# A deformable-convolution block: the first pair's weight products ahead of the second pair's offset convolution, batch norm operations and second grid later on DVE

## Chip, cores and metric

One NeuronCore of a Trainium2 chip runs one program. The metric is the device time of one execution, in microseconds (us); lower is better. Engines are named as in the profile: PE (TensorE; PEld its weight loads), DVE (VectorE), ACT (ScalarE), POOL (GpSimd), SP (SyncE, whose queue issues most DMAs).

## What is computed

Two residual bottleneck blocks on x of shape (4, 256, 16, 16). Only the middle of the first is touched by the change: a 3x3 convolution gives offsets and a mask, a deformable 3x3 convolution samples with them.

```python
out = relu(group_norm(conv(x, w1)))                # 64 channels
om = conv(out, w_off, pad=1) + b_off               # 27 channels
off_x, off_y, mask = om[:, :9], om[:, 9:18], sigmoid(om[:, 18:])
py, px = grid_y + off_y, grid_x + off_x
sampled = bilinear_sample(out, py, px) * mask      # 9 taps
out = einsum('bckhw,ock->bohw', sampled, w2)
out = relu(group_norm(out)); out = group_norm(conv(out, w3)); x = relu(out + x)
# second block: 16-bit quantised activations, power-of-two weights:
# 1x1, depthwise 3x3, batch norm, relu, 3x3, batch norm, relu, 1x1, batch norm, + x, relu
```

## The kernel before

The four images are laid out as two pairs (`b2` 0 and 1); within a pair the two images are the halves `h`, on partitions 0 to 63 and 64 to 127. Every engine has its program written out by hand, and semaphores are all that orders the engines against each other. An engine runs its own list strictly in order.

Bilinear sampling is done as matrix products. A **unit** `i` (0 to 7) is a tile `t = i // 2` (pair `t // 2`, 128 of its 256 pixels) and a half `h`. For each tile DVE makes `differences(t)` (offset coordinate minus pixel coordinate) and from them the hat functions `hats`, in y and x; `apply_mask(t)` multiplies the sigmoid mask into one of them. For each unit `make_g(i)` multiplies the two hats out into `g_rows` (9 taps by 256 source pixels), called g(i) below. PE transposes it in thirds of three taps, `turn(n)`, into one of the three double banks `slot`, ACT copies each third to `g_cols` (`copy_g(n)`), and PE multiplies `g_cols` with `v_sb` and sums into `acc` (`sample(t, first_tap, last_tap)`). For tiles 0 and 1 DVE makes the hats alone; for tiles 2 and 3 ACT does the second half of it (`distance(2)`, `distance(3)`), between its copies.

`v_sb` holds the **weight products**: features times w2, eight products v0 to v7 (`make_v(i)`, 128x512, eight taps of one pair, pixel half and image) and eight small ones for the ninth tap (`make_last_v(i)`). A product uses 64 rows of the PE array, those of its half `i % 2`. PE writes them to PSUM, ACT copies them (`copy_v(i)`, and two copies for the ninth tap).

The **offsets** of a pair: `om_step(b2, s)` (five steps) is the offset convolution; of its result ACT copies the upper 64 partitions (`copy_om_rest`), and DVE adds the grid to the lower ones (`add_grid`). `om_turn(b2)` transposes the sum on PE; its result is copied to `omt_sb` (DVE for the first pair, ACT in `copy_omt(1)` for the second), and ACT makes the mask. In the kernel before, PE runs both offset convolutions one after the other with `om_turn(0)` inside the second, then v0 to v3, `om_turn(1)`, and the rest of the products, and only then the turns. The second pair's offsets lie in the second banks of `slot[0]` and `slot[1]`.

The six **batch norm operations** (`bn_std`, `bn_inv`, `bn_off`, `bn_minus`) are DVE work on 128x4 elements or less, needed only in the second block. In the kernel before they stand right after `add_grid(0)`.

Later on DVE: `moments(0)` and `pair_scale(3, 0)` normalise the first pair, five operations quantise the weights (`wq_mag`, `wqb`), and `eight_moments(0)` takes the moments of `conv3(0)`; PE waits for these in `eight_means(0)`, between two stretches of sampling of tile 3.

Of the kernel before, what the change touches and what calls it, by code (L numbers as in the profile page):

```python
# [38 lines left out]
P = 128  # L39
# [75 lines left out]
def build(nc, x, first, pairs, consts, woff, grid, w2, w3, wq, out):  # L115
    with ExitStack() as ctx:
# [233 lines left out]
        def _(pe):  # L350
# [35 lines left out]
            def om_step(b2, s):  # L386
                for p in range(2):
                    k = s + TAPS_A * p
                    if k < TAPS:
                        mm = nc.tensor.matmul(slot[0][CB * p:CB * p + CB, BANK * b2:BANK * b2 + N],  # L390
# [4 lines left out]
            def om_turn(b2):  # L395
# [10 lines left out]
            for b2 in range(B2):  # L406
                pe.wait_ge(feat_ready, b2 + 1)
                for s in range(TAPS_A):
                    mm = om_step(b2, s)
                    if b2 == 1 and s == 1:  # L410
                        pe.wait_ge(consts_in, 16)
                        om_turn(0)
                mm.then_inc(om_done, 1)

            v_banks = [small[0], small[1], acc[0][:], acc[1][:]]
            pe.wait_ge(w2_in, 16)

            def make_v(i):  # L420
                b2, q, h = i // 4, i // 2 % 2, i % 2
                pe.wait_ge(flat_ready, b2 + 1)
                if i >= 4:

                    pe.wait_ge(v_ready, i - 3)
                at = N * b2 + P * q
                lhs = feat_flat[rows(h), at:at + P]
                nc.tensor.matmul(v_banks[i % 4], lhs, w2_sb[rows(h), 0:BANK], start=True, stop=True
                                 ).then_inc(v_done, 1)

            def make_last_v(i):
                b2, q, h = i // 4, i // 2 % 2, i % 2
# [12 lines left out]
            mm.then_inc(v_done, 1)


            def turn(n):
# [176 lines left out]
        def _(a):  # L625
# [587 lines left out]
```

## Time and profile before

| what | value |
|---|---|
| time, median of 3 runs (lowest to highest) | 92.92 us (92.44 to 93.06) |
| time of the profiled execution | 93.05 us |
| its span in the trace | 91.27 us |
| PE, DVE, ACT busy | 75.5, 67.0, 51.1 us |

The span is what the trace shows between first and last instruction; the time has some 1.8 us around it. Busy times overlap, since the engines run side by side. Matmuls are pipelined and their ends are modelled. The trace leaves buffer numbers out, so `w_sb` is w2 or w3, and `slot` any of the three.

### The profile page before, as it was taken

Reading aid. Unit: us, or ns where it says so; the run is one execution under the profiler, and the core shown is the slowest. Engines: PE = TensorE matmul, PEld = TensorE weight load, DVE = VectorE, ACT = ScalarE, POOL = GpSimd, SP = SyncE. Lnnn points to the kernel's source line nnn. Section 1 sums busy time; section 2 is a strip of 40 time slices with the busy share of each in tenths; the row PEclk is TensorE's granted clock in tenths of the full one; section 3 lists DMA queues with packets and bytes.
Section 4 is the critical chain, followed back from the end, with each engine's and each line's share of the span. In section 5 each row is a group of like instructions: output and inputs, shape, how many; then the busy total and the mean of one; then the engine's idle time right before and its main releaser. Section 6 shows DMA issues by size and latency. Waiting matters only on the chain.

```text
span 91.3 us, 2176 instructions
## 1 busy us (share of the span) xinstructions
PE 75.5 (83%) x886; PEld 51.3 (56%) x886; DVE 67.0 (73%) x182; ACT 51.1 (56%) x92; POOL 5.0 (6%) x10
## 2 busy tenths in 40 slices
PE   4999999995899898999999989967359889896400
PEld 1325665564798878798996964452214385572100
DVE  1225449999999599995799437977898875849950
ACT  4102374879948999994792015336363343744760
POOL 7500110000000000000003100000000000000000
PEclk9999999999999999999999999999999999999975
DMA  1999800000000000000000000000000000000076
GB/s 21 317 337 292 334 4 0 0 0 7 0 7 0 0 7 0 7 7 0 0 7 0 0 0 7 0 0 0 0 0 0 0 0 0 7 4 0 0 245 215
DMA packets 3274, 4.17 MB, mean 46 GB/s; under 512 B 256, under 2 KB 2688, under 8 KB 3264
## 3 DMA queue, kind: packets, MB, share of 16 engines
q1 hardware_dynamic: 2992, 3.76, 12.8%
q10 hardware_dynamic: 272, 0.26, 0.8%
q8 instruction: 7, 0.11, 0.5%
q14 instruction: 3, 0.02, 0.1%
HBM read 2.98 MB, written 1.05 MB: 44 GB/s over the span
## 4 chain that ended last, share of the span: by engine, by line
PE 49%; DVE 32%; ACT 10%; issue 4%; DVEq 0%; ACTq 0%
PE acc L475 15%; PE slot L462 9%; DVE g_rows L886 8%; PE slot L354 6%; PE acc L604 5%; PE acc L365 3%; DVE g_cols L1040 3%; PE slot L390 3%; ACT g_cols L704 2%; DVE g_cols L984 2%; ACT g_cols L788 2%; PE slot L539 2%; ACT pad L757 2%; DVE g_cols L1130 2%; DVE stats L948 2%
## 5 line engine op out<-in xcount | busy, mean ns | idle before, releaser
L886 DVE TENSOR_TENSOR g_rows<-hats 128x2304 f32<-128x2304 f32 (+1 forms) x12 | 20.6, 1752 | 0.1
L704 ACT ACTIVATE g_cols<-slot 128x768 f32<-128x768 f32 x24 | 17.8, 830 | 3.7 <-PE slot L462 3.7
L475 PE MATMUL acc<-g_cols,v_sb 128*64 128x128 f32 x288 | 17.9, 277 | 0.0
L475 PEld LDWEIGHTS acc<-g_cols,v_sb 128*64 128x64 f32 x288 | 15.5, 137 | 1.1 <-issue 0.3
L354 PE MATMUL slot<-zeros 128*128 128x512 bf16 x54 | 15.1, 412 | 1.2 <-DVE zeros L807 1.2
L462 PE MATMUL slot<-consts_sb,g_rows 64*128 64x64 f32 x288 | 11.8, 226 | 2.1 <-DVE g_rows L886 1.7
L462 PEld LDWEIGHTS slot<-consts_sb,g_rows 64*128 64x128 f32 x288 | 10.3, 139 | 3.9 <-DVE g_rows L886 2.6
L354 PEld LDWEIGHTS slot<-zeros 128*128 128x128 bf16 x54 | 5.4, 107 | 7.3 <-issue 2.6
L757 ACT ACTIVATE pad<-g_cols 64x256 bf16<-64x256 int8 x8 | 3.3, 418 | 4.6 <-DVE g_cols L1040 4.5
L817 DVE BATCH_NORM_STATS2 stats<-acc 128x6 f32<-128x256 f32 x4 | 1.7, 428 | 5.2 <-PE acc L365 2.6
L539 PE MATMUL slot<-consts_sb,mx 128*128 128x128 f32 x12 | 3.2, 319 | 2.3 <-DVE mx L991 2.0
L390 PE MATMUL slot<-feat,woff_sb 128*64 128x256 f32 x36 | 4.7, 385 | 0.0
L635 ACT ACTIVATE std<-var,eps_sb 128x1 f32<-128x1 f32 x4 | 1.2, 297 | 6.1 <-DVE var L824 6.1
L539 PEld LDWEIGHTS slot<-consts_sb,mx 128*128 128x128 f32 x12 | 1.8, 176 | 4.0 <-DVE mx L991 2.5
L780 ACT ACTIVATE act<-raw,bn_off 128x256 f32<-128x256 f32 x4 | 2.0, 508 | 2.8 <-DVE mx L1116 2.8
L390 PEld LDWEIGHTS slot<-feat,woff_sb 128*64 128x64 f32 x36 | 2.7, 135 | 1.2
L734 ACT ACTIVATE g_cols<-g_cols 128x512 f32<-128x512 f32 x2 | 1.3, 631 | 3.6 <-DVE piece_max L984 3.6
L1116 DVE CUSTOM_DVE_ANT_0 raw<-acc,bn_mul,bn_minus 128x256 f32<-128x256 f32 x4 | 1.9, 482 | 1.7 <-DVE bn_mul L1124 0.9
L345 POOL TENSOR_TENSOR pegq<-consts_sb,wqb 128x576 bf16<-128x576 f32 x1 | 1.1, 1149 | 37.2 <-DVE wqb L942 37.2
L757 ACT ACTIVATE g_cols<-g_cols 128x512 bf16<-128x512 int8 x4 | 2.4, 625 | 1.3 <-DVE g_cols L1040 1.2
L855 DVE TENSOR_TENSOR hats<-omt_sb,consts_sb 128x576 f32<-128x576 f32 x4 | 3.0, 752 | 0.0
L984 DVE CUSTOM_DVE_ANT_0 g_cols<-g_cols,x_sb 128x256 f32<-128x256 f32 x8 | 3.0, 417 | 0.1
(140 smaller groups left out, 117.6 us busy)
## 6 DMA issues: line engine op xcount, KB each, us to landing
out<-g_cols SPq DMA_DIRECT2D x4, 256.0 KB, 2.3
x_sb<-x SPq DMA_DIRECT2D x3, 256.0 KB, 4.4
wq_sb<-wq SPq DMA_DIRECT2D x1, 484.5 KB, 6.3
woff_sb<-woff SPq DMA_DIRECT2D x1, 288.0 KB, 5.5
w_sb<-w SPq DMA_DIRECT2D x1, 288.0 KB, 5.5
x_sb<-x ACTq DMA_DIRECT2D x1, 256.0 KB, 3.1
w_sb<-w SPq DMA_DIRECT2D x1, 256.0 KB, 6.4
consts_sb<-consts SPq DMA_DIRECT2D x1, 232.0 KB, 5.4
```

The source lines that it names most:

```text
L354: nc.tensor.matmul(bank, zeros[:, 0:P], zeros[:], start=True, stop=True)
L365: mm = nc.tensor.matmul(acc[b2][rows(h), 0:N], w1_sb[:, c, :], x_sb[:, c, b2, h, :], start=(c == 0), stop=(c == CH - 1))
L390: mm = nc.tensor.matmul(slot[0][CB * p:CB * p + CB, BANK * b2:BANK * b2 + N], woff_sb[:, k, :], window(feat, b2, k), start=(s == 0), stop= ...
L462: mm = nc.tensor.transpose(slot[SLOT_OF[n % TURNS]][:, BANK * r + at:BANK * r + at + CB], g_rows[i % 3][rows(r), k, ROWS_Q * q:ROWS_Q * q ...
L475: mm = nc.tensor.matmul(acc[b2][rows(h), at:at + P], v_sb[:, B2 * h + b2, q, k, :], g_cols[t][h][:, NQ * k + q, :], start=(k == 0 and q == ...
L539: nc.tensor.matmul(spread[b2] if biased else small[b2][:, P:2 * P], mx[:, n, b2:b2 + 1].to_broadcast([P, P]), ident, start=not biased, sto ...
L604: mm = nc.tensor.matmul(acc[b2][rows(h), 0:N], weights(k), window(pad[:, b2], h, k), start=(k == 0), stop=(k == TAPS - 1))
L704: nc.scalar.activation(dst.rearrange("p k (r n) -> p k r n", r=HALVES), src.rearrange("p r (k n) -> p k r n", k=per), ACT.Copy).then_inc(g ...
L757: nc.scalar.activation(dst, src, ACT.Copy, scale=256.0).then_inc(hi_ready, 1)
L855: return tt(hats[:, t].rearrange("p h a k y -> p h (a k) y"), omt_sb[:, t // NQ, t % NQ, :, 0:2 * TAPS].unsqueeze(3).to_broadcast([P, HALV ...
L886: tt(g_rows[i % 3][:, taps], hats[:, t, h, 1, taps].unsqueeze(3).to_broadcast(shape), hats[:, t, h, 0, taps].unsqueeze(2).to_broadcast(sha ...
L984: last = nc.vector.tensor_tensor_reduce(y0[:, c, b2, h, :], y0[:, c, b2, h, :], x_sb[:, c, b2, h, :], 1.0, 0.0, ALU.add, ALU.max, piece_ma ...
```

## The change

On PE, v0 now comes before `om_turn(0)`, then v1 to v3 and all eight ninth-tap products; the second pair's offset convolution comes after v4, with v5 after its third step and v6 behind it. `om_turn(1)` moves behind `sample(0, 0, 4)`, and v7 behind `sample(0, 5, 6)`. The wait for w2's transfer moves ahead of the first offset convolution. The second pair's offsets and their transpose go to the bank `acc[1]`; v4, v5 and v6 use `acc[0]`, v7 `acc[1]`. The ninth-tap products go to the first banks of `slot[0]` and `slot[1]`. ACT's copies follow that order. On DVE the batch norm operations move behind `pair_scale(3, 0)`, and `add_grid(1)` behind `make_g(1)`. No instruction is added or taken away.

```diff
+        def om_of(b2, p):
+            return (slot[0] if b2 == 0 else acc[1])[rows(p), 0:N]
+        def omt_of(b2):
+            return (slot[1] if b2 == 0 else acc[1])[:, 0:NQ * CB]
+        v_banks = (small[0], small[1], acc[0][:], acc[1][:], acc[0][:], acc[0][:], acc[0][:], acc[1][:])
+        def last_v_of(h):
+            return slot[h][:, 0:T * CB]
...
             pe.wait_ge(woff_in, 16)
-            for b2 in range(B2):
-                pe.wait_ge(feat_ready, b2 + 1)
-                for s in range(TAPS_A):
-                    mm = om_step(b2, s)
-                    if b2 == 1 and s == 1:
-                        pe.wait_ge(consts_in, 16)
-                        om_turn(0)
-                mm.then_inc(om_done, 1)
-            v_banks = [small[0], small[1], acc[0][:], acc[1][:]]
             pe.wait_ge(w2_in, 16)
             def make_v(i):
                 b2, q, h = i // 4, i // 2 % 2, i % 2
                 pe.wait_ge(flat_ready, b2 + 1)
-                if i >= 4:
-                    pe.wait_ge(v_ready, i - 3)
                 at = N * b2 + P * q
                 lhs = feat_flat[rows(h), at:at + P]
-                nc.tensor.matmul(v_banks[i % 4], lhs, w2_sb[rows(h), 0:BANK], start=True, stop=True
+                nc.tensor.matmul(v_banks[i], lhs, w2_sb[rows(h), 0:BANK], start=True, stop=True
                                  ).then_inc(v_done, 1)
             def make_last_v(i):
                 b2, q, h = i // 4, i // 2 % 2, i % 2
-                at = BANK * h + CB * (i // 2)
-                return nc.tensor.matmul(slot[0][:, at:at + CB], feat_flat[rows(h), N * b2 + P * q:N * b2 + P * q + P],
+                at = CB * (i // 2)
+                return nc.tensor.matmul(last_v_of(h)[:, at:at + CB], feat_flat[rows(h), N * b2 + P * q:N * b2 + P * q + P],
                                         w2_sb[rows(h), BANK:TAPS * CB], start=True, stop=True)
-            for i in range(4):
-                make_v(i)
-            om_turn(1)
-            for i in range(4):
-                make_last_v(i)
-            for i in range(4, 2 * T):
-                make_v(i)
+            pe.wait_ge(feat_ready, 1)
+            for s in range(TAPS_A):
+                mm = om_step(0, s)
+            mm.then_inc(om_done, 1)
+            make_v(0)
+            pe.wait_ge(consts_in, 16)
+            om_turn(0)
+            make_v(1)
+            make_v(2)
+            pe.wait_ge(feat_ready, 2)
+            make_v(3)
+            pe.wait_ge(omt_ready, 1)
+            pe.wait_ge(flat_ready, B2)
+            for i in range(2 * T):
                 mm = make_last_v(i)
             mm.then_inc(v_done, 1)
+            pe.wait_ge(v_ready, 3)
+            make_v(4)
+            pe.wait_ge(v_ready, 4)
+            for s in range(TAPS_A):
+                mm = om_step(1, s)
+                if s == 2:
+                    pe.wait_ge(v_ready, 6)
+                    make_v(5)
+            mm.then_inc(om_done, 1)
+            pe.wait_ge(v_ready, 7)
+            make_v(6)
...
-                    pe.wait_ge(v_ready, (5, 6, 2 * T + 1)[n])
+                    pe.wait_ge(v_ready, 5)
...
             turns(0, 5)
             sample(0, 0, 4)
+            om_turn(1)
             turns(6, 8)
             sample(0, 5, 6)
+            pe.wait_ge(omt_ready, 2)
+            make_v(7)
...
             copy_om_rest(0)
             nc.scalar.preload_act_table(ACT.Sigmoid)
             make_mask(0)
-            copy_om_rest(1)
-            for i in range(2 * T):
+            for i in range(4):
                 copy_v(i)
-                if i == 3:
-                    copy_omt(1)
-            a.wait_ge(v_done, 2 * T + 1)
+            a.wait_ge(v_done, 5)
             for h in range(HALVES):
                 last = nc.scalar.activation(v_sb[:, B2 * h:B2 * h + B2, :, V_MAIN, :],
-                                            slot[0][:, BANK * h:BANK * h + T * CB].rearrange(
-                                                "p (b q o) -> p b q o", b=B2, q=NQ), ACT.Copy)
+                                            last_v_of(h).rearrange("p (b q o) -> p b q o", b=B2, q=NQ), ACT.Copy)
             last.then_inc(v_ready, 1)
+            for i in range(4, 7):
+                copy_v(i)
+            copy_om_rest(1)
...
+                if n == 5:
+                    copy_omt(1)
                 if n == 8:
+                    copy_v(7)
                     distance(2)
...
             add_grid(0)
-            dve.wait_ge(bn_std_ready, 1)
-            settle(nc.vector.reciprocal(bn_std[:], bn_std[:]))
-            settle(tt(bn_inv[:], bn_std[:], vec[:, V_BNG:V_BNG + 4], ALU.mult))
-            settle(tt(bn_off[:], bn_inv[:], vec[:, V_BNM:V_BNM + 4], ALU.mult))
-            settle(tt(bn_off[:], vec[:, V_BNB:V_BNB + 4], bn_off[:], ALU.subtract))
-            settle(stt(bn_off[:, 0:1], bn_inv[:, 0:1], vec[:, V_PEGB:V_PEGB + 1], bn_off[:, 0:1], ALU.mult, ALU.add))
-            settle(ts(bn_minus[:], bn_off[:, 0:2], -1.0, None, ALU.mult))
             dve.wait_ge(omt_done, 1)
-            nc.vector.tensor_copy(omt_sb[:, 0].rearrange("p q h o -> p (q h o)"), slot[1][:, 0:NQ * CB]
+            nc.vector.tensor_copy(omt_sb[:, 0].rearrange("p q h o -> p (q h o)"), omt_of(0)
                                   ).then_inc(omt_ready, 1)
             settle(differences(0))
             make_hats(0)
-            add_grid(1)
             apply_mask(0)
             make_g(0)
             make_g(1)
+            add_grid(1)
             settle(differences(1))
             make_hats(1)
             apply_mask(1)
...
             pair_scale(3, 0, V_GN2S, V_GN2B)
+            dve.wait_ge(bn_std_ready, 1)
+            settle(nc.vector.reciprocal(bn_std[:], bn_std[:]))
+            settle(tt(bn_inv[:], bn_std[:], vec[:, V_BNG:V_BNG + 4], ALU.mult))
+            settle(tt(bn_off[:], bn_inv[:], vec[:, V_BNM:V_BNM + 4], ALU.mult))
+            settle(tt(bn_off[:], vec[:, V_BNB:V_BNB + 4], bn_off[:], ALU.subtract))
+            settle(stt(bn_off[:, 0:1], bn_inv[:, 0:1], vec[:, V_PEGB:V_PEGB + 1], bn_off[:, 0:1], ALU.mult, ALU.add))
+            settle(ts(bn_minus[:], bn_off[:, 0:2], -1.0, None, ALU.mult))
             dve.wait_ge(wq_in, 16)
...
```

PE around the offset convolutions, before (`feat,woff_sb` is the convolution, `consts_sb,om_sb` is `om_turn`, `w2_sb,feat_flat` a weight product, 128x512 a large one, 128x64 a ninth-tap one):

```order
L390 MATMUL slot0<-feat,woff_sb 64x256 [waits feat_ready,woff_in]
L390 MATMUL slot0<-feat,woff_sb 64x256 x8
L390 MATMUL slot0<-feat,woff_sb 64x256 [waits feat_ready]
L390 MATMUL slot0<-feat,woff_sb 64x256 x3
L401 MATMUL slot1<-consts_sb,om_sb 128x64 [waits om_rest_ready,om_ready,consts_in]
L401 MATMUL slot1<-consts_sb,om_sb 128x64
L390 MATMUL slot0<-feat,woff_sb 64x256 x5
L428 MATMUL slot2<-w2_sb,feat_flat 128x512 [waits flat_ready,w2_in]
L428 MATMUL slot2<-w2_sb,feat_flat 128x512 [waits flat_ready]
```

and after:

```order
L404 MATMUL slot0<-feat,woff_sb 64x256 [waits feat_ready,w2_in,woff_in]
L404 MATMUL slot0<-feat,woff_sb 64x256 x8
L427 MATMUL slot2<-w2_sb,feat_flat 128x512 [waits flat_ready]
L415 MATMUL slot1<-consts_sb,om_sb 128x64 [waits om_rest_ready,om_ready,consts_in]
L415 MATMUL slot1<-consts_sb,om_sb 128x64
L427 MATMUL slot2<-w2_sb,feat_flat 128x512 [waits flat_ready]
L427 MATMUL acc0<-w2_sb,feat_flat 128x512 [waits flat_ready]
L427 MATMUL acc1<-w2_sb,feat_flat 128x512 [waits flat_ready,feat_ready]
```

The first convolution matmul has w2 among its waits, one large product stands between the first convolution and its turn, and the second convolution has left this place.

PE further on, before (`consts_sb,g_rows` are turns of 12, `g_cols,v_sb` is sampling):

```order
L462 MATMUL slot<-consts_sb,g_rows 128x64 x72
L475 MATMUL acc<-g_cols,v_sb 64x128 x20
L462 MATMUL slot<-consts_sb,g_rows 128x64 x36
L475 MATMUL acc<-g_cols,v_sb 64x128 x8
L462 MATMUL slot<-consts_sb,g_rows 128x64 x36
```

and after, from v4 on:

```order
L427 MATMUL acc<-w_sb,feat_flat 128x512
L404 MATMUL acc<-feat,woff_sb 64x256 x6
L427 MATMUL acc<-w_sb,feat_flat 128x512
L404 MATMUL acc<-feat,woff_sb 64x256 x3
L427 MATMUL acc<-w_sb,feat_flat 128x512
L479 MATMUL slot<-consts_sb,g_rows 128x64 x72
L492 MATMUL acc<-g_cols,v_sb 64x128 x20
L415 MATMUL acc<-consts_sb,om_sb 128x64 x2
L479 MATMUL slot<-consts_sb,g_rows 128x64 x36
L492 MATMUL acc<-g_cols,v_sb 64x128 x8
L427 MATMUL acc<-w_sb,feat_flat 128x512
```

The second convolution stands between v4, v5 and v6; its turn comes after 20 matmuls of sampling, and v7 after 8 more.

ACT, before, from the second `copy_om_rest` on:

```order
L651 ACTIVATE om_sb<-slot 64x256
L678 ACTIVATE v_sb<-slot 128x512 x2
L678 ACTIVATE v_sb<-acc 128x512 x2
L661 ACTIVATE omt_sb<-slot 128x128
L656 ACTIVATE mask<-omt_sb 128x36
L678 ACTIVATE v_sb<-slot 128x512 x2
L678 ACTIVATE v_sb<-acc 128x512 x2
L692 ACTIVATE v_sb<-slot 128x4x64 x2
L704 ACTIVATE g_cols<-slot 128x768 x9
L669 ACTIVATE hats<-hats 128x576
L671 ACTIVATE hats<-hats,one_sb 128x576
L704 ACTIVATE g_cols<-slot 128x768 x3
```

and after, from the first mask on:

```order
L676 ACTIVATE mask<-omt_sb 128x36
L696 ACTIVATE v_sb<-slot 128x512 x2
L696 ACTIVATE v_sb<-acc 128x512 x2
L706 ACTIVATE v_sb<-slot 128x4x64 x2
L696 ACTIVATE v_sb<-acc 128x512 x3
L671 ACTIVATE om_sb<-acc 64x256
L720 ACTIVATE g_cols<-slot 128x768 x6
L681 ACTIVATE omt_sb<-acc 128x128
L676 ACTIVATE mask<-omt_sb 128x36
L720 ACTIVATE g_cols<-slot 128x768 x3
L696 ACTIVATE v_sb<-acc 128x512
L689 ACTIVATE hats<-hats 128x576
```

Ahead of the copies of g there are one product copy and the second pair's transposed offsets less; these now stand between copies of g, the product right ahead of `distance(2)`.

## Rows read from the trace of the kernel before

**Rows 1.** The page's first part: busy time, share of the span, instructions.

```profile
...
PE 75.5 (83%) x886; PEld 51.3 (56%) x886; DVE 67.0 (73%) x182; ACT 51.1 (56%) x92; POOL 5.0 (6%) x10
...
```

**Rows 2.** The chain that ended last, 9 to 32: start us, length us, what.

```profile
...
13.89 0.18 DVE bn_minus L900
...
16.95 5.04 DVE g_rows L886 x2
...
24.83 2.40 PE acc L475 x40
...
27.79 2.21 ACT g_cols L704 x3
...
```

**Rows 3.** The DMA issues; w2 is the 288 KB row: KB, us to landing.

```profile
...
w_sb<-w SPq DMA_DIRECT2D x1, 288.0 KB, 5.5
...
```

**Rows 4.** Instructions in order of time, 4.8 to 13.8: start, length, engine, line.

```profile
...
4.84 0.43 SPq L322 DMA_DIRECT2D w_sb<-w  x1
...
9.94 3.24 PE L390 MATMUL slot<-feat,woff_sb 128*64 128x256 f32 x26
...
12.35 0.38 ACT L651 ACTIVATE om_sb<-slot 64x256 f32<-64x256 f32 x1 [0.56 <-PE slot L390]
12.45 0.48 DVE L848 SCALAR_TENSOR_TENSOR om_sb<-slot,first_sb,grid_sb 64x256 f32<-64x256 f32 x1 [1.27 <-PE slot L390]
12.74 1.28 ACT L682 ACT_TABLE_LOAD   x1
...
13.10 0.66 PE L401 MATMUL slot<-consts_sb,om_sb 128*128 128x64 f32 x4
...
13.69 1.51 PE L390 MATMUL slot<-feat,woff_sb 128*64 128x256 f32 x10
...
```

**Rows 5.** The same view, 15.1 to 21.9.

```profile
...
15.13 1.13 PE L428 MATMUL slot<-w_sb,feat_flat 64*128 64x512 f32 x4
...
15.71 0.46 DVE L864 TENSOR_SCALAR hats<-hats 128x576 f32<-128x576 f32 x1
...
16.29 1.08 ACT L678 ACTIVATE v_sb<-slot 128x512 f32<-128x512 f32 x2 [0.68 <-PE slot L428]
16.48 0.44 DVE L873 TENSOR_TENSOR hats<-hats,mask 128x288 f32<-128x288 f32 x1
...
17.05 0.66 PE L401 MATMUL slot<-consts_sb,om_sb 128*128 128x64 f32 x4
...
18.13 1.13 PE L428 MATMUL slot<-w_sb,feat_flat 64*128 64x512 f32 x4
18.21 0.31 ACT L661 ACTIVATE omt_sb<-slot 128x128 f32<-128x128 f32 x1
18.56 0.23 ACT L656 ACTIVATE mask<-omt_sb 128x36 f32<-128x36 f32 x1
...
19.24 1.09 ACT L678 ACTIVATE v_sb<-slot 128x512 f32<-128x512 f32 x2 [0.45 <-PE slot L428]
...
21.82 4.36 ACT L704 ACTIVATE g_cols<-slot 128x768 f32<-128x768 f32 x6
...
```

**Rows 6.** The same view, 26.6 to 31.5.

```profile
...
26.64 0.75 DVE L855 TENSOR_TENSOR hats<-omt_sb,consts_sb 128x576 f32<-128x576 f32 x1
...
27.16 1.33 PE L462 MATMUL slot<-consts_sb,g_rows 64*128 64x64 f32 x36
...
29.88 0.70 ACT L669 ACTIVATE hats<-hats 128x576 f32<-128x576 f32 x1
...
31.42 0.46 DVE L873 TENSOR_TENSOR hats<-hats,mask 128x288 f32<-128x288 f32 x1 [0.90 <-ACT hats L671]
...
```

**Rows 7.** The same view, 43.8 to 52.1, from two stretches.

```profile
...
43.86 0.29 DVE L824 TENSOR_SCALAR var<-acc 128x1 f32<-128x1 f32 x1 [1.54 <-PE acc L373]
...
51.07 0.25 DVE L952 BATCH_NORM_AGGREGATE mv<-stats 128x2 f32<-128x6 f32 x2
...
52.00 0.39 PE L519 MATMUL slot<-mv,consts_sb 128*128 128x4 f32 x2
...
```

More of the change, by code:

```diff
@@ L389, in om_step @@
                     if k < TAPS:
-                        mm = nc.tensor.matmul(slot[0][CB * p:CB * p + CB, BANK * b2:BANK * b2 + N],
+                        mm = nc.tensor.matmul(om_of(b2, p),
                                               woff_sb[:, k, :], window(feat, b2, k), start=(s == 0),
@@ L400, in om_turn @@
                     at = N * b2 + P * q
-                    mm = nc.tensor.matmul(slot[1][:, BANK * b2 + CB * q:BANK * b2 + CB * q + CB],
+                    mm = nc.tensor.matmul(omt_of(b2)[:, CB * q:CB * q + CB],
                                           om_sb[:, at:at + P], fold, start=True, stop=True)
@@ L650, in copy_om_rest @@
                 a.wait_ge(om_done, b2 + 1)
-                nc.scalar.activation(om_sb[CB:P, N * b2:N * b2 + N], slot[0][CB:P, BANK * b2:BANK * b2 + N],
+                nc.scalar.activation(om_sb[CB:P, N * b2:N * b2 + N], om_of(b2, 1),
                                      ACT.Copy).then_inc(om_rest_ready, 1)
@@ L661, in copy_omt @@
                 nc.scalar.activation(omt_sb[:, b2].rearrange("p q h o -> p (q h o)"),
-                                     slot[1][:, BANK * b2:BANK * b2 + NQ * CB], ACT.Copy).then_inc(omt_ready, 1)
+                                     omt_of(b2), ACT.Copy).then_inc(omt_ready, 1)
                 make_mask(b2)
@@ L671, in distance @@
                 nc.scalar.activation(v, v, ACT.Relu, bias=one_sb[:, 0:1], scale=-1.0).then_inc(relu1_ready, 1)
-            v_banks = [small[0], small[1], acc[0][:], acc[1][:]]
             def copy_v(i):
                 b2, q, h = i // 4, i // 2 % 2, i % 2
-                a.wait_ge(v_done, i + 1)
+                a.wait_ge(v_done, i + 1 + (i >= 4))
                 nc.scalar.activation(v_sb[:, B2 * h + b2, q, 0:V_MAIN, :].rearrange("p k o -> p (k o)"),
-                                     v_banks[i % 4], ACT.Copy).then_inc(v_ready, 1)
+                                     v_banks[i], ACT.Copy).then_inc(v_ready, 1)
             copy_om_rest(0)
@@ L847, in add_grid @@
                 dve.wait_ge(om_done, b2 + 1)
-                stt(om_sb[0:CB, N * b2:N * b2 + N], slot[0][0:CB, BANK * b2:BANK * b2 + N],
+                stt(om_sb[0:CB, N * b2:N * b2 + N], om_of(b2, 0),
                     vec[0:CB, V_BOFF:V_BOFF + 1], grid_sb[:, N * b2:N * b2 + N], ALU.add, ALU.add
```

## Prediction

> **What bounds the kernel now.** I read the busy shares first, then the chain that ended last, then the instructions in order of time around the edit, last the DMA issues. PE (83%) and DVE (73%) are both well filled [rows 1], so the shares alone decide nothing. The chain shows the stage that the edit touches. Up to 22 us it runs mostly over DVE: batch norm, hats, the two 2.5 us products g(0) and g(1). Then PE samples, and from 27.79 it goes through ACT: three copies of transposed products, and then through tile 2's hats [rows 2]. The instructions in time order say the same: DVE waits 0.90 for ACT before the mask of tile 2 at 31.42, after which g(4) starts at 31.9 [rows 6]. So until 32 us the path depends on when ACT is free and when the second pair's offsets reach it and DVE. From 34.5 us the order of the three engines is unchanged. After `pair_sums(3, 0)` DVE has a chain of its own, and PE asks for its end only at 52.00 [rows 7].
>
> I sum at the level of the trace (span 91.27, time 93.05, which is 0.13 above the median 92.92).
>
> **A wait that moved.** PE now waits for w2 ahead of the first pair's offset convolution. That convolution started at 9.94 [rows 4]. w2 was issued at 4.84 [rows 4] and landed 5.5 later [rows 3], at about 10.34. Before, its first user was at 15.13 [rows 5], so nobody noticed. **+0.40** at the start of the chain, for PE, and through it for ACT and DVE. If the landing comes 0.4 earlier, zero.
>
> **First pair's offsets.** The convolution is done for ACT at 12.35 + 0.40 = 12.75, for DVE's `add_grid` at 12.85, which ends at 13.33. PE fills the gap with v0. Then `om_turn(0)` starts at about 13.4 and takes 0.59 until the next PE instruction (13.10 to 13.69), 0.66 to its end [rows 4]: 14.07. DVE copied it at 14.1 before, because the six batch norm operations stood there until 14.07 [rows 2]. Before, the turned offsets were there at 13.76, so these six hid all but 0.34 of themselves; now that 0.34 goes to the late w2. Omt copy at 14.1: **0**. `add_grid(1)` leaves the place ahead of mask(0) and gives about 0.28 (the hats ended at 16.17, the mask started at 16.48 [rows 5]), so g(0) starts at 16.67 instead of 16.95. After g(1) the grid returns with 0.40, so differences(1) is at 22.0, 0.12 late, and g(2) ends at about 26.85, where differences(2) stood at 26.64 [rows 6]. DVE by itself is thus nearly unmoved.
>
> **What one product v costs alone.** PE issues a product every 0.48 (four between 15.13 and `om_turn(1)` at 17.05), and a small one every 0.12 (four between 17.64, when that turn is issued, and 18.13) [rows 5]. But ACT, idle, could copy v0 only at 16.29, 1.16 after its start, and v4, started at 18.13, at 19.24, 1.11 after [rows 5]. In both cases the next product, on the other 64 rows, was under way. Two products in 0.96 with a latency of 1.13 fit an overlap on the two halves, each taking about 0.86. Alone, then, 0.86 of PE; the other bound is 0.48. I take 0.86, since the latency was measured twice. After the change v0, v4, v5, v6 and v7 stand alone; v1 with v2, and v3 with the small ones, don't. The Trainium skill says the same in TensorE: Matmul & The Clock Gate, Part 3: matmuls on different row groups of the array run concurrently. This trace agrees, with the latencies 1.16 and 1.11; by that rule the lone products pay double, and if it didn't hold here the time would be about 0.4 less.
>
> **PE and ACT until the first copy of g.** v1 and v2 run from 14.0 to 14.95, v3 and eight small products of 0.12 to about 16.3. ACT's table load (1.28) [rows 4] now starts at 13.14 and ends at 14.42, mask(0) at 14.7; copies of v follow each other at 0.49 (x2 in 1.08) and last 0.60 [rows 5]: the third ends at 16.3, and v4 may start. v4 to 17.2; three steps of the second offset convolution at 0.44 each (seven steps lie between 9.94 and 13.10 [rows 4]) to 18.5; v5 to 19.35; two steps to 20.2. v6 waits for ACT's copy of v5: 18.5 + 1.13 + 0.60 = 20.25. ACT starts to copy v6 at 20.25 + 1.13 = 21.4, the second offset rest at 21.9, and g's first copy at 22.2, where 21.82 stood [rows 5]: **+0.4**. With v at 0.48 it is 21.8. This is the surprise of the edit: ACT loses one v copy and the omt copy here, 1.1 us of work, yet gains nothing, because it now waits for single products.
>
> **Second pair's offsets.** `om_turn(1)` now stands behind `sample(0, 0, 4)`, which needs five of ACT's copies. Sample started 3.0 after the first copy (24.83) [rows 2] and held PE 2.33, to 27.16 [rows 6]; now 25.2 to 27.55. The turn takes 0.59, ACT sees it at 28.25, copies (0.31) and makes the mask (0.23) [rows 5]: differences(2) at 28.6, mask done at 28.85. Before, this was all over at 18.8. DVE has g(2) done at 26.85 and stands still for 1.75. Behind that wait are g(3), differences(3), mask(2), g(4): everything of DVE. ACT's copies 6 to 8 start at 28.85 instead of 27.79 and take 2.09 (27.79 to 29.88) [rows 2, 6], to 30.95. Then **copy_v(7)**, new in this place. PE has done turns 6 to 8 by 29.45 (1.3 [rows 6]) and sampled two taps by 30.35 (8 of the 20 pairs that took 2.33), v7 starts then and is ready 1.13 later, at 31.4, ACT copies (0.49) and starts tile 2's distance at 31.9; before 29.88 [rows 6]. The path through DVE (differences(2) 1.96 late, but 0.9 of idle time before the mask) is shorter. So g(4), the next piece of the chain, is **+2.0** late, the 0.4 and 0.4 included. After it PE, ACT and DVE have the same work in the same order, and PE has no gap to give it back: it is busy from turn to turn.
>
> **Batch norm's new place.** Six operations, 1.14 from the first grid's end at 12.93 to 14.07 [rows 2, 4], 1.2 with the bit that overlaps the grid, now ahead of the `wq` work. DVE's chain starts at 43.86 with PE's sums and ends with the moments at 51.32; PE takes them at 52.00 [rows 7], so the slack is 0.68 less 0.05 of wake-up. 1.2 - 0.63 = **+0.6**. Both sides hang on the same `pair_sums`, so an earlier delay doesn't change it. Behind PE's wait are the last samples of tile 3 and all after it. Bounds: 0 (if PE came 0.6 late too) and 1.2.
>
> **Sum.** 2.0 + 0.6 = 2.6: 93.05 + 2.6 = 95.65, I say **95.6**. With the lower ends (v 0.48: -0.4; w2 on time: -0.4) it is 94.8; with small products not overlapping v3, and 0.2 more at each of the three handoffs of v4, v5, v6, 96.5.
>
> **Rivals.** *ACT does get ahead.* If a product alone is ready sooner than 1.13 after its start (say 0.65: no partner to share with), v6 is copied about 1.1 earlier and g's first copy is at 21.1. Then the turn of the second pair is at 26.45, differences(2) at 27.5, copies 6 to 8 at 27.79 as before, and v7's copy adds 0.5: +0.5, with batch norm +1.1: 94.15. For it: nowhere in the trace does a product stand alone. Against: both latencies agree, and they don't depend on what ran before. Chance 0.17. *The other side, faster.* The front gain of DVE (0.28, or 0.67 if w2 is on time) lasts if differences(2) is ready at g(2)'s end. That needs the turned second pair by 26.1, sample from 22.8, g's first copy by 19.8: two microseconds before its time today. With batch norm hidden it would give 93.05 - 0.67 = 92.4, with it 93.0. PE's work alone (20.2 above) speaks against it. Chance 0.10 for this and for all mixtures near no change, under half of it faster. *Worse.* Each handoff PE to ACT to PE on v4, v5, v6 is serial, and a PE that waits for g(3) (32.0) could push v7 and the turns further: above 96.8, chance 0.10. My forecast keeps 0.63. A difference under 1% (0.9 us) can't be told from none in this kernel: slower by over 1% 0.80, within 0.14, faster 0.06. The range reaches into the first rival and stops short of the worst: 94.0 to 96.8.
>
> **What would show it.** First offset matmul at about 10.3, not 9.9. DVE's g(0) near 16.7. ACT's first copy of g near 22.2 (21.1 if the first rival holds). DVE idle ahead of differences(2) for 1.5 to 2 us, and the chain running through `om_turn(1)` and ACT's omt copy. ACT waiting for v7. PE idle about 0.6 ahead of `eight_means(0)`, its releaser DVE's moments. I am wrong if ACT starts copying g before 21, or if DVE goes from g(2) into differences(2) without a gap.

## Result: slower by 5.0%, where 2.9% was forecast

The changed kernel takes 98.69 us (median of 4 runs, 97.23 to 100.97), the kernel before 92.88 beside it: 1.050 times the time, 95% interval 1.045 to 1.055. The forecast was 95.6, in a range of 94.0 to 96.8. The direction was right, the size was not, and the time lies outside the range. The ratio leaves out executions more than 1.5% above the fastest of the same kernel, so of the changed kernel it takes 97.23 and 98.05 alone, while 98.69 is the median of all four. The profiled execution of the changed kernel is the longest of the four, 100.97 us with a span of 99.2, and its mean granted clock is 0.948, against 0.984 in the run of 97.23.

Lines below are of the changed kernel's profile. First PE's start, from the instructions in order of time and the DMA issues, beside [rows 3, 4]:

```profile
w_sb<-w SPq DMA_DIRECT2D x1, 288.0 KB, 6.4
```

```profile
4.83 0.43 SPq L336 DMA_DIRECT2D w_sb<-w  x1
...
11.31 2.35 PE L404 MATMUL slot<-feat,woff_sb 128*64 128x256 f32 x18 [0.63 <-issue]
...
14.64 0.66 PE L415 MATMUL slot<-consts_sb,om_sb 128*128 128x64 f32 x4
...
17.55 0.69 PE L427 MATMUL acc<-w_sb,feat_flat 64*128 64x512 f32 x1
...
18.60 1.52 PE L404 MATMUL acc<-feat,woff_sb 128*64 128x256 f32 x12
...
20.04 1.12 PE L427 MATMUL acc<-w_sb,feat_flat 64*128 64x512 f32 x2
...
21.10 1.08 PE L404 MATMUL acc<-feat,woff_sb 128*64 128x256 f32 x6
21.20 0.60 ACT L696 ACTIVATE v_sb<-acc 128x512 f32<-128x512 f32 x1 [1.90 <-PE acc L427]
...
23.26 0.60 ACT L696 ACTIVATE v_sb<-acc 128x512 f32<-128x512 f32 x1 [1.46 <-PE acc L427]
...
24.29 4.33 ACT L720 ACTIVATE g_cols<-slot 128x768 f32<-128x768 f32 x6
```

w2 lands at 4.83 + 6.4 = 11.23, the convolution starts at 11.31, where 9.94 stood [rows 4]. That isn't all w2. The last product of the group norm's pair sums stands right ahead of the convolution, first in the kernel before, then in the changed one:

```profile
9.64 0.36 PE L373 MATMUL slot<-mv,pairs_sb 128*128 128x1 f32 x2
```

```profile
10.32 0.36 PE L387 MATMUL slot<-mv,pairs_sb 128*128 128x1 f32 x2
```

In all six profiled kernels that don't wait for w2 here, the convolution starts 0.29 or 0.30 behind the start of that product. So the changed kernel would have started at about 10.61 in this execution, 0.67 late because the last part of x landed late, and the wait for w2 added 0.70.

v4 alone holds PE from 17.55 to 18.60, 1.05 us, and v5 from 20.04 to 21.10, 1.06. ACT, 1.90 and 1.46 idle, waits for v5 and v6, and its first copy of g comes at 24.29, where 21.82 stood [rows 5].

The same view further on, beside [rows 2, 6, 7]:

```profile
27.26 4.07 PE L492 MATMUL acc<-g_cols,v_sb 128*64 128x128 f32 x40
31.26 0.66 PE L415 MATMUL acc<-consts_sb,om_sb 128*128 128x64 f32 x4
...
32.27 0.76 DVE L874 TENSOR_TENSOR hats<-omt_sb,consts_sb 128x576 f32<-128x576 f32 x1 [4.18 <-ACT omt_sb L681]
32.48 2.21 ACT L720 ACTIVATE g_cols<-slot 128x768 f32<-128x768 f32 x3
...
35.30 0.60 ACT L696 ACTIVATE v_sb<-acc 128x512 f32<-128x512 f32 x1 [0.60 <-PE acc L427]
...
37.80 5.03 DVE L905 TENSOR_TENSOR g_rows<-hats 128x2304 f32<-128x2304 f32 x2
...
58.46 0.39 PE L539 MATMUL slot<-mv,consts_sb 128*128 128x4 f32 x2 [0.48 <-DVE mv L971]
```

The 40 sampling matmuls take 4.07 us, where the same 40 took 2.40 [rows 2]. Nothing in the program changed for them. The view by stretches shows their clock (start and end, length, busy time of PE, PEld, DVE, ACT and POOL with instructions, PE's granted clock, DMA share, GB/s):

```profile
24.00:25.00 1.00, 0.35 (x10) 0.21 (x6) 0.93 (x3) 0.98 (x3) 0.00 (x0) 1.00 0.00 0
25.00:26.00 1.00, 0.65 (x14) 0.57 (x15) 0.93 (x3) 1.00 (x3) 0.00 (x0) 1.00 0.00 0
26.00:27.00 1.00, 0.89 (x23) 0.78 (x24) 1.00 (x1) 1.00 (x2) 0.00 (x0) 1.00 0.00 0
27.00:28.00 1.00, 0.98 (x18) 0.84 (x16) 1.00 (x1) 1.00 (x3) 0.00 (x0) 0.76 0.00 0
28.00:29.00 1.00, 1.00 (x12) 1.00 (x10) 0.09 (x1) 0.61 (x1) 0.00 (x0) 0.50 0.00 0
29.00:30.00 1.00, 1.00 (x14) 1.00 (x12) 0.00 (x0) 0.00 (x0) 0.00 (x0) 0.50 0.06 16
```

From 27.5 on PE is granted half of its clock, the 1.2 GHz level, until 31.0. Ahead of that it had been busy for 0.35 of one microsecond and 0.65 of the next, since its fourth turn waited for ACT's late first copy of g. In the profile's line of granted clock this happens twice, while the profiled execution of the kernel before has nothing of the kind until its last microseconds. First the changed kernel:

```profile
PEclk9999999999957999999999999589999999999985
```

then the kernel before:

```profile
PEclk9999999999999999999999999999999999999975
```

The second stretch, 61.6 to 65.1, lies on the eight filler matmuls ahead of `conv3(1)`, which both kernels have, and costs 1.5 us (below). The kernel before isn't free of such falls: in 5 of the 26 runs that it had beside the experiments its mean granted clock was 0.948 to 0.963, at 94.46 to 95.21 us.

**Where the time went.** Five milestones cut the span: the start of the first offset convolution, ACT's first copy of g, DVE's start of g(4), PE's start of `eight_means(0)`, and the first `mx` matmul. Before: 9.94, 21.82, 31.91, 52.00, 61.45. After: 11.31, 24.29, 37.80, 58.46, 69.40. The stretches grow by 1.37, 1.10, 3.42, 0.57 and 1.49, in sum 7.95, and the profiled times differ by 7.92. Of the 3.42, 4.07 - 2.40 = 1.67 is the clock, so 1.75 is order. Of the first 1.37, 0.67 is the late part of x (above), which is no part of the change.

### The profile page after: what moved, and what is told of

The parts are those of the page before. It is cut to its first block, busy times and chain, and to the rows that moved or that the text cites. A ratio compares the mean times of both kernels' runs of the same rounds, so it can differ in the third digit from the quotient of the medians.

```text
span 99.2 us, 2177 instructions
## 1 busy us (share of the span) xinstructions
PE 82.4 (83%) x886; PEld 53.9 (54%) x886; DVE 67.2 (68%) x182; ACT 51.6 (52%) x92; POOL 5.0 (5%) x10
## 3 DMA queue, kind: packets, MB, share of 16 engines
q1 hardware_dynamic: 2992, 3.76, 11.7%
HBM read 2.98 MB, written 1.05 MB: 41 GB/s over the span
## 4 chain that ended last, share of the span: by engine, by line
PE 49%; DVE 27%; ACT 8%; DMA 6%; issue 4%; SPq 2%; DVEq 0%; ACTq 0%
PE acc L492 11%; PE slot L479 7%; DMA x_sb<-x 6%; PE acc L624 5%; PE acc L427 4%; DVE g_rows L905 4%; PE acc L368 3%; DVE stats L967 3%; DVE g_cols L1059 3%; PE acc L404 2%; PE slot L404 2%; PE slot L427 2%; DVE g_cols L1003 2%; PE slot L368 2%; ACT g_cols L807 2%
## 5 line engine op out<-in xcount | busy, mean ns | idle before, releaser
L492 PE MATMUL acc<-g_cols,v_sb 128*64 128x128 f32 x288 | 19.7, 293 | 0.1
L492 PEld LDWEIGHTS acc<-g_cols,v_sb 128*64 128x64 f32 x288 | 17.2, 147 | 1.3 <-ACT g_cols L720 0.5
L427 PE MATMUL acc<-w_sb,feat_flat 64*128 64x512 f32 x12 | 6.5, 632 | 0.0
L696 ACT ACTIVATE v_sb<-acc 128x512 f32<-128x512 f32 x6 | 3.5, 602 | 4.0 <-PE acc L427 4.0
L379 PE MATMUL acc<-x_sb,first_sb 128*64 128x256 f32 x16 | 3.3, 526 | 0.4 <-DMA x_sb<-x 0.4
L368 PE MATMUL acc<-zeros 128*128 128x512 bf16 x8 | 3.5, 618 | 0.0
```

The costliest lines, as they stand in the source:

```text
L368: nc.tensor.matmul(bank, zeros[:, 0:P], zeros[:], start=True, stop=True)
L379: mm = nc.tensor.matmul(acc[b2][rows(h), 0:N], w1_sb[:, c, :], x_sb[:, c, b2, h, :], start=(c == 0), stop=(c == CH - 1))
L427: nc.tensor.matmul(v_banks[i], lhs, w2_sb[rows(h), 0:BANK], start=True, stop=True).then_inc(v_done, 1)
L492: mm = nc.tensor.matmul(acc[b2][rows(h), at:at + P], v_sb[:, B2 * h + b2, q, k, :], g_cols[t][h][:, NQ * k + q, :], start=(k == 0 and q == ...
L696: nc.scalar.activation(v_sb[:, B2 * h + b2, q, 0:V_MAIN, :].rearrange("p k o -> p (k o)"), v_banks[i], ACT.Copy).then_inc(v_ready, 1)
```

## Experiments

The stretches behind the start repeat to 0.1 us or so between kernels that have the same order in them, which makes a table possible. All in us, from each kernel's profiled execution; "g" is the stretch from the convolution's start to the first copy of g, "g(4)" the next, without the 1.67 of the clock where the 40 matmuls took 4.07, "means" the next, "mx" the last. "Median" is over all runs of a kernel (4 each, 10 of y2_before_bn_late). Beside the three groups of experiments the kernel before gave medians of 93.12, 93.13 and 93.13. The start depends also on when x lands: in the profiled run of x5_pairs it is 10.65 with no wait for w2.

| kernel | w2 lands | start | g | g(4) | 40 matmuls | means | mx | median |
|---|---|---|---|---|---|---|---|---|
| before | 10.34 | 9.94 | 11.88 | 10.09 | 2.40 | 20.09 | 9.45 | 92.88 |
| after | 11.23 | 11.31 | 12.98 | 11.84 | 4.07 | 20.66 | 10.94 | 98.69 |
| y1_before_w2_early | 10.63 | 10.71 | 11.86 | 10.09 | 2.40 | 20.09 | 9.45 | 94.47 |
| y2_before_bn_late | 10.64 | 10.00 | 11.89 | 10.09 | 2.40 | 20.64 | 9.46 | 94.02 |
| x1_w2_back | 9.74 | 9.57 | 13.01 | 11.86 | 4.07 | 20.65 | 10.99 | 99.45 |
| x2_bn_front | 10.64 | 10.70 | 13.09 | 11.85 | 4.07 | 20.09 | 9.45 | 98.62 |
| x3_turn_early | 10.34 | 10.45 | 12.97 | 11.76 | 2.40 | 20.65 | 9.45 | 97.84 |
| x4_all_back | 10.34 | 9.60 | 13.11 | 10.56 | 2.40 | 20.58 | 9.45 | 94.80 |
| x5_pairs | 11.24 | 10.65 | 12.09 | 10.55 | 4.07 | 20.57 | 9.46 | 95.02 |
| x6_fill | 10.24 | 10.30 | 12.97 | 11.85 | 2.40 | 20.65 | 9.46 | 96.76 |
| x7_fill_first | 10.84 | 10.92 | 12.97 | 11.85 | 2.40 | 20.66 | 10.97 | 98.03 |
| x8_pairs_fill | 10.34 | 10.39 | 12.07 | 11.85 | 2.40 | 20.66 | 9.45 | 96.24 |
| x9_back_fill | 10.34 | 10.01 | 12.09 | 10.56 | 2.40 | 21.02 | 9.35 | 94.71 |

**The wait for w2 alone, in the kernel before** (y1_before_w2_early).

```diff
             pe.wait_ge(woff_in, 16)
+            pe.wait_ge(w2_in, 16)
```

> The kernel before with one thing of the change alone: PE waits for w2 ahead of the first offset convolution. Wait theory: the convolution starts at w2's landing, 0.1 to 0.7 us after the time at which PE is ready for it, and the whole time grows by as much, 0.3 to 0.6 (93.2 to 93.5). If the front has slack that takes it up: within 0.1 of the kernel before.

Measured: 94.47 (94.05 to 95.25), ratio 1.017, interval 1.008 to 1.026. The convolution starts at 10.71, 0.08 after w2's landing, 0.77 late, and nothing gives it back (11.86, 10.09, 20.09). The rest of the profiled run's loss, 0.67 behind the `mx` milestone, comes with a fall of the clock from 67.2 to 70.7 us. In all seven kernels with this wait the start follows the landing by 0.05 to 0.11; the same 288 KB, issued at 4.83 or 4.84 each time, land after 5.4 to 6.4.

**The batch norm operations alone, in the kernel before** (y2_before_bn_late).

```diff
             pair_scale(3, 0, V_GN2S, V_GN2B)
+            dve.wait_ge(bn_std_ready, 1)
+            settle(nc.vector.reciprocal(bn_std[:], bn_std[:]))
...
+            settle(ts(bn_minus[:], bn_off[:, 0:2], -1.0, None, ALU.mult))
```

and the same six taken away behind `add_grid(0)`.

> The kernel before with the six batch norm operations alone moved behind pair_scale(3, 0). Two effects: DVE's omt copy comes 0.34 us earlier, and g(0) with it; PE waits 0.5 to 0.6 for the moments in eight_means(0). Slack theory: net +0.2 to +0.3 if the front gain reaches the chain, +0.6 if it does not, since that chain then runs through ACT (93.1 to 93.5). Rival: no change, or faster.

Measured: ratio 1.008, interval 1.005 to 1.012 (0.75 us), and 20.64 - 20.09 = 0.55 in the stretch "means".

**The wait for w2 back** (x1_w2_back): from ahead of the first convolution to ahead of `make_v(0)`.

> The changed kernel with one thing undone: PE waits for w2 only ahead of v0, not ahead of the first offset convolution. Wait theory: the convolution starts when the pair sums are done (10.0 to 10.7), 0.4 to 0.7 us earlier than in the changed kernel, and since every engine hangs on it the time falls by as much, to about 97.1 from 97.6. Rival: the gap in front is absorbed by v0 and the late products, time within 0.3 of the changed kernel.

Measured: 99.45 (99.45 to 99.53), ratio 1.069, interval 1.063 to 1.076: higher, not lower. The start is at 9.57, 1.74 ahead of the changed kernel's, about 1.0 of it because x landed earlier. But the clock falls twice in the profiled run, and the other three have the same mean clock (0.947 or 0.948) and the same time, where two of the changed kernel's four runs have 0.972 and 0.984. So the medians of the two don't tell what the wait is worth. The sum still closes: -0.37 start, 1.13, 1.77, 1.67 clock, 0.56, 1.54 make 6.30, and 93.05 + 6.30 = 99.35.

**Batch norm operations back at the front** (x2_bn_front).

> The changed kernel with the six batch norm operations back ahead of the omt copy. Slack theory: PE no longer waits for DVE's moments before eight_means(0), 0.5 to 0.6 us less; at the front the operations cost nothing, since DVE waits there over 1 us for the turned offsets. About 97.1. Clock theory adds: the half-clock stretch after eight_means(0) (61.6 to 65 in the changed kernel, some 1.5 us) comes from that PE wait and goes with it; then up to 2 us less against the slow runs. Rival: 0.3 or less, because DVE's omt copy gets later by as much.

Measured: 98.62 (96.27 to 98.92); no ratio, since three of the four runs have a clock of 0.950 to 0.955. "means" is back at 20.09, 0.57 gained, at the price of 0.11 in "g". The 40 matmuls take 4.07 again. The second fall hasn't gone with PE's wait, as the expectation had it: it lies at 71.4 to 74.8 us. So the wait ahead of `eight_means(0)` isn't needed for a second fall.

**The second pair's turn ahead of the sampling** (x3_turn_early).

```diff
             turns(0, 5)
-            sample(0, 0, 4)
             om_turn(1)
+            sample(0, 0, 4)
...
-                if n == 5:
+                if n == 4:
                     copy_omt(1)
```

> The changed kernel with om_turn(1) ahead of sample(0, 0, 4) instead of behind it, and ACT's copy of its result after the fifth copy of g instead of the sixth. Theory that the late second offsets are the cost: DVE's wait ahead of differences(2) (4.2 us) shrinks to under 1, g(3) comes 2.5 to 4 us earlier; what is left is bounded by ACT's first copy of g, so the time falls by 1.5 to 2.5, to 95.2 to 96.2. Rival, that ACT's late start with g sets everything: time falls by 0.5 or less.

Measured: 97.84 (96.90 to 98.83), ratio 1.048, interval 1.034 to 1.062. DVE's 4.18 us wait for the turned offsets is gone, as the instructions in order of time show:

```profile
26.31 0.66 PE L415 MATMUL acc<-consts_sb,om_sb 128*128 128x64 f32 x4
26.90 2.40 PE L492 MATMUL acc<-g_cols,v_sb 128*64 128x128 f32 x40
...
27.31 0.76 DVE L874 TENSOR_TENSOR hats<-omt_sb,consts_sb 128x576 f32<-128x576 f32 x1
...
29.86 2.21 ACT L720 ACTIVATE g_cols<-slot 128x768 f32<-128x768 f32 x3 [1.62 <-PE slot L479]
...
32.68 0.60 ACT L696 ACTIVATE v_sb<-acc 128x512 f32<-128x512 f32 x1 [0.60 <-PE acc L427]
...
34.69 0.46 DVE L892 TENSOR_TENSOR hats<-hats,mask 128x288 f32<-128x288 f32 x1 [3.48 <-ACT hats L691]
```

Yet "g(4)" is 11.76 instead of 11.84. DVE now waits 3.48 for ACT at the mask, and ACT waits for PE's turns and for v7. The path runs over PE and ACT. Of the 4.18, 1.67 was the clock's fall on the 40 matmuls; the other 2.51, the most striking wait of the changed kernel's trace, costs 0.08 us.

**Four parts back at once** (x4_all_back): w2, batch norm, the early turn, and on ACT `copy_v(7)` two copies of g later, behind `distance(2)`.

```diff
                 if n == 8:
-                    copy_v(7)
                     distance(2)
+                if n == 10:
+                    copy_v(7)
```

> The changed kernel with four things undone together: w2's wait, the batch norm operations, om_turn(1) ahead of the sampling, and v7's copy by ACT moved from ahead of distance(2) to after the eleventh copy of g. What stays is the order of the products, the late second offset convolution and add_grid(1) behind g(1). If the four are additive: 0.5 + 0.6 + 2 + 0.5 = 3.6 less, about 94. If the late products and the second convolution cost nothing by themselves, 93 or less.

Measured: 94.80 (94.67 to 94.90), ratio 1.019, interval 1.013 to 1.025. Against x3_turn_early "g(4)" falls from 11.76 to 10.56: `copy_v(7)` ahead of `distance(2)` costs 1.20, of which the copy is 0.60 and the wait for v7 0.60. (The two kernels differ in the wait for w2 and the batch norm operations too, but x1_w2_back and x2_bn_front show that these leave "g(4)" at 11.86 and 11.85.) Later it costs 0.48 in "means". With no fall of the clock the sum is -0.34 + 1.23 + 0.47 + 0.49 = 1.85, and the profiled time 94.90 is 1.85 above 93.05.

**v4 and v5 as a pair** (x5_pairs, on the kernel of x4).

```diff
-        v_banks = (small[0], small[1], acc[0][:], acc[1][:], acc[0][:], acc[0][:], acc[0][:], acc[1][:])
+        v_banks = (small[0], small[1], acc[0][:], acc[1][:], acc[0][:], small[1], acc[0][:], acc[1][:])
...
             make_v(4)
+            make_v(5)
             pe.wait_ge(v_ready, 4)
             for s in range(TAPS_A):
                 mm = om_step(1, s)
-                if s == 2:
-                    pe.wait_ge(v_ready, 6)
-                    make_v(5)
...
```

> The version with four things undone (94.8), and in it v5 directly after v4, in a bank of its own, instead of inside the second offset convolution. Theory that a product alone holds PE for 1.05 us where two on different halves take about 1.0 together: PE is done with v6 about 0.9 to 1.0 us earlier, ACT's first copy of g comes 0.7 to 1.0 earlier, and the time is 93.8 to 94.1. Rival (a product costs 0.48 wherever it stands): copy of g within 0.2, time unchanged.

Measured: 95.02 (94.43 to 96.61), ratio 1.020, interval 1.013 to 1.026. "g" falls from 13.11 to 12.09: two lone products and their handoff cost 1.02 more than the same two as a pair.

```profile
17.02 0.69 PE L426 MATMUL acc<-w_sb,feat_flat 64*128 64x512 f32 x1
...
17.25 0.65 PE L426 MATMUL slot<-w_sb,feat_flat 64*128 64x512 f32 x1
...
18.25 2.37 PE L404 MATMUL acc<-feat,woff_sb 128*64 128x256 f32 x18
```

The pair holds PE for 18.25 - 17.02 = 1.23, where the two alone took 2.11. (v5 also has another bank here. The bank isn't what makes a lone product dear: v0, in a bank of `slot`, held PE as long as v4 and v5 in `acc[0]`.) The profiled time doesn't follow, for two reasons: the last part of x landed late, so the start is 1.05 behind that of x4_all_back, and the clock falls on the 40 matmuls, which takes 1.67. 1.05 - 1.02 + 1.66 = 1.69, and 96.61 - 94.90 = 1.71. Between the two kernels' ratios, 1.020 and 1.019, the gain can't be seen.

**Two fillers in the changed kernel** (x6_fill), at places where PE waits, each ahead of a stretch at half clock.

```diff
-            turns(0, 5)
+            turns(0, 2)
+            pe.wait_ge(v_ready, 8)
+            idle(4, acc[0][:])
+            turns(3, 5)
...
             sample(3, 2, 6)
+            idle(2, small[1])
             eight_means(0)
```

> The changed kernel with idle matmuls on zeros in two places where PE waits: four ahead of turn(3), two ahead of eight_means(0). They add nothing to the result. Clock theory, that short waits of PE in a stretch of half-filled matmuls let its clock fall: no half-clock stretch in the sampling at 27 to 31 us nor at 61 to 65, the four runs have granted clocks of 0.98 and times of 96.8 to 97.3. Rival, that the falls have nothing to do with these waits: clocks still between 0.95 and 0.98 in most runs, times of 98 and more.

Measured: 96.76 (96.57 to 96.91), ratio 1.041, interval 1.037 to 1.045, with a mean clock of 0.981 to 0.988 in all four runs. More work, 1.9 us less than the changed kernel's median, and a ratio of 1.041 against 1.050:

```profile
24.00:25.00 1.00, 0.89 (x16) 0.55 (x16) 0.94 (x2) 1.00 (x3) 0.00 (x0) 1.00 0.00 0
25.00:26.00 1.00, 0.89 (x23) 0.78 (x24) 1.00 (x1) 1.00 (x2) 0.00 (x0) 1.00 0.00 0
...
26.00:28.00 2.00, 1.98 (x40) 1.84 (x37) 1.08 (x1) 1.60 (x3) 0.00 (x0) 1.00 0.00 0
```

PE is busy for 0.89 where it had 0.35 and 0.65, and the 40 matmuls take 2.40. All other stretches are the changed kernel's to 0.02. So this is the changed kernel without its falls: +0.36, 1.09, 1.76, 0.56, in sum 3.77 to 3.78, and 96.80 measured in the profiled run against 93.05 + 3.78 = 96.83.

This shows what the falls cost, not yet what brings them. x4_all_back and x5_pairs have nearly the same pause of PE ahead of the 40 matmuls, and the clock stays in the first and falls in the second. The stretch of the pause and the next, x4_all_back first, then x5_pairs:

```profile
23.00:24.00 1.00, 0.34 (x11) 0.37 (x12) 0.93 (x3) 1.00 (x2) 0.00 (x0) 1.00 0.00 0
24.00:25.00 1.00, 0.84 (x20) 0.59 (x16) 1.00 (x1) 1.00 (x3) 0.00 (x0) 1.00 0.00 0
```

```profile
23.00:24.00 1.00, 0.30 (x9) 0.33 (x11) 0.94 (x2) 1.00 (x2) 0.00 (x0) 1.00 0.00 0
24.00:25.00 1.00, 0.88 (x22) 0.63 (x17) 0.92 (x2) 1.00 (x3) 0.00 (x0) 1.00 0.00 0
```

And x3_turn_early and y2_before_bn_late have the changed kernel's wait ahead of `eight_means(0)` without a filler, and no fall in the 14 us behind it. So the second filler isn't shown to be what keeps the clock there.

**The first filler alone** (x7_fill_first).

> The changed kernel with the first of the two fillers alone: four matrix products of zeros ahead of the fourth turn (turn 3), in the time in which TensorE waits for ScalarE's first copy of g; nothing ahead of the second stretch (eight_means of pair 0). Theory that each fall of TensorE's clock comes from TensorE's own pauses ahead of it: the first sampling products (40 of them) take 2.40 us again and not 4.07, the second stretch keeps its half clock, mean granted clock about 0.966, time 96.8 (both fillers) + 1.5 = 98.3 us. Rival, that the two fillers did nothing to the clock and the run with both of them was in luck four times: both falls return, clock about 0.948, 99 to 101 us in some of the runs. Third way: the second fall hung on the first alone, then 96.8 us with a clock of 0.98.

Measured: 98.03, ratio 1.044, interval 1.039 to 1.048, from runs of 97.08, 97.08, 98.98 and 99.56 (clock 0.985, 0.980, 0.963, 0.937). The profiled one, 98.98, is as the first theory has it: the 40 matmuls at 2.40, the second fall present, "mx" 10.97. But two runs, by their time and clock, have no fall there, so the second isn't certain without its filler, and one has lost more than one fall costs.

**The pair and both fillers, on the changed kernel** (x8_pairs_fill).

> The changed kernel with both fillers (96.76 us measured) and one part more undone: the weight product v5 directly behind v4, in a bank of its own, where the changed kernel runs both alone, 1.05 us each, with twelve products of the offset convolution between them. Theory that the path goes from the weight products to ScalarE's first copy of g and from there through TensorE: two products as a pair took 0.95 less, the first copy of g comes 12.1 us behind the start of the first offset convolution and not 12.97, VectorE's g(4) at +24.0 and not +24.8, time 96.76 - 0.9 = 95.9 us. Rival, that VectorE's wait for the second pair's turned offsets (which stays behind the 40 sampling products here) sets it by itself: nothing gained, 96.7 us.

Measured: 96.24 (96.03 to 96.89), ratio 1.036, interval 1.031 to 1.041; "g" is 12.07, and since "g(4)" stays 11.85, DVE's g(4) comes 0.90 earlier too. DVE's wait for the turned offsets shrinks from 2.51 in x6_fill to 1.60. This agrees with the path through ACT's first copy of g. It doesn't tell ACT from DVE behind it, since the second pair's turned offsets come 0.90 earlier too; x3_turn_early told that.

**Everything back but the place of the second convolution** (x9_back_fill).

> Everything undone that can be with the offset convolution of the second pair left behind the weight products: wait for w2 behind the first offset convolution, batch norm operations at the front, second turn of offsets ahead of the sampling, last copy of v late, v4 and v5 as a pair, and both fillers. Measured without fillers: 95.02 us with the clock falling in some runs. Theory: first copy of g 0.2 us later than before, sampling 0.67 us later (the second turn of offsets stands ahead of it), no fall of the clock, so 92.9 + 0.7 to 0.9 = 93.6 to 93.8 us, ratio 1.007 to 1.01, still no gain over the kernel before. Rival, that the order has a gain of its own that the waits had hidden (VectorE reaches the second pair's grid in time): 92.5 us or less.

Measured: 94.71 (94.27 to 95.27), ratio 1.017, interval 1.012 to 1.021. That is 0.9 to 1.1 above what I expected. `copy_v(7)` late (0.48) and the second filler (0.45 against x5_pairs, here where PE has no wait to cover it) make "means" 21.02, which I had left out, and in the profiled run the clock falls from 68.0 to 71.4 us, with both fillers in place. No version beat the kernel before, so none is recommended.

## Why the prediction was wrong

Two steps failed. The step to ACT's first copy of g put nothing beyond the wait for w2, and 1.1 us were there: a lone product was sized at 0.86 us of PE and held it 1.05, and the handoffs PE, ACT, PE behind it made the rest. And the sum had no term for PE's clock, whose two falls cost 3.2 us in the profiled run. By the prediction's own steps, sizes without the clock, from the table:

- **The w2 wait.** Forecast +0.40 from a landing at 10.34. The mechanism is right (the start follows the landing by 0.05 to 0.11), the size is a matter of the run and mostly larger. Counted from where the convolution would have started without it (0.29 behind the last pair sum), the wait costs 0.30 in x6_fill and 0.69 to 0.89 in the six others, 0.70 of them in the profiled run, where the other 0.67 of the +1.37 is x. I took one landing time as fixed.
- **Omt copy 0.** It came 15.34 - 11.31 = 4.03 behind the convolution's start, not 14.1 - 10.34 = 3.76, since `om_turn(0)` had to wait for the whole of v0 (1.05). g(0) still began 6.63 behind that start, where 7.01 stood [rows 2, 4]. DVE's gain of 0.38 was worth nothing, as forecast.
- **Products alone, and the first copy of g.** This is the term that was furthest off. Forecast 22.2, nothing beyond the w2 wait; measured +1.10 beyond it. Counted from the convolution's start, v4 came at 6.24 (forecast 5.96), lasted 1.05 (0.86), three convolution steps 1.44 (1.3), v5 1.06 (0.86), two steps 1.01 (0.88), so v6 at 10.80 instead of 9.91. ACT then needed 1.03 and not 0.8 between the starts of v6's copy and g's. I deduced 0.86 from a latency of 1.13 and a pace of 0.48; a lone product really holds PE 1.05, more than twice its share in a row of four (0.48) and 1.7 times its share of the pair in x5_pairs (0.61). The other bound that I gave (0.48) was on the wrong side.
- **Second pair's offsets, v7.** Forecast from the first copy of g to g(4): 33.9 - 22.2 = 11.7; measured 11.84 and 11.85. The size is right, and the path I had named was half right: v7's copy ahead of `distance(2)` costs 1.20 (x4 against x3), the late turn of the offsets itself 0.08. In x3_turn_early, ACT's copies 6 to 8 wait for PE's turns and not for the turned offsets.
- **Batch norm +0.6.** Measured 0.55 to 0.57, in three comparisons.
- **Sum.** 2.6 forecast; without falls of the clock the changed kernel has 3.8 (x6_fill), 96.8, the top of my range. 1.1 of the difference is the first copy of g. In x6_fill w2 landed early; the changed kernel's own run with a clock of 0.984 took 97.23.
- **What had no term: PE's clock.** Two falls cost 1.67 and 1.5 us in the profiled run, and the median is 98.69 where x6_fill, with a clock of 0.981 to 0.988 in every run, has 96.76. The profile before showed full clock up to its last microseconds, and I took that as given in a change that makes PE wait for ACT. The fillers speak for it that the falls hang on what PE does there: none of the four runs of x6_fill has one, and with the first filler the 40 matmuls took 2.40 in all four profiles. It isn't shown, since x4_all_back has the pause and no fall. When one comes stays open.
- **Rivals.** "ACT does get ahead" fell: its first copy of g came later, not earlier. "Worse" named the serial handoffs PE, ACT, PE on v4, v5, v6, and they did cost more, but by themselves they reach only 96.8, its lower edge; that the time went clearly above it is the clock, which it didn't name.
- **What would show it.** DVE's idle time before differences(2) was to be 1.5 to 2; it was 4.18, or 2.51 with the clock held (x6_fill).

In the prediction I drew on the Trainium skill, TensorE: Matmul & The Clock Gate, Part 3 (matmuls on different row groups run concurrently). The trace agrees, and more strongly than I used it: 1.05 us of PE alone, 0.48 apiece in a row of four on alternating halves [rows 5], 0.61 apiece in the pair of x5_pairs.

## What to carry to other kernels

Moving half-array products apart to fill gaps raised the price of one from 0.48 or 0.61 us to 1.05, and each became a serial handoff; move them in pairs. Look at the granted clock by stretches before any wait is explained, and ask of a change that makes TensorE wait more what a fall would cost: here 1.5 to 1.7 us each. A wait of 2.51 us was worth 0.08. Don't put a transfer that nobody waited for in front of the first work: its landing varied by 1.5 us between executions.

## Not expected of the hardware

- The granted clock fell to half for about 3.5 us at a time in a kernel whose PE is 83% busy; ahead of the first fall lay microseconds in which it was busy for 0.35 and 0.65. Forty sampling matmuls then take 4.07 instead of 2.40.
- A kernel with a wait taken away can come out slower this way: x1_w2_back starts 1.74 us earlier than the profiled run of the changed kernel, and its median is 0.76 higher, since all four of its runs have a clock of 0.947 or 0.948. With four filler matmuls in PE's wait, the 40 matmuls took 2.40 again.
- The same DMA of 288 KB, issued at the same time, landed after 4.9 to 6.4 us in thirteen profiled executions.
